# A two-layer relational graph network with two attentions on one core: five places for messages instead of two

## What is computed

```python
def _rgcn_conv(x, src, dst, etype, W, root, b):
    seg = dst * num_rel + etype
    sums = segment_sum(x[src], seg)                      # one sum per node and relation
    cnt = segment_sum(ones, seg)
    mean = sums / maximum(cnt, 1.0)[:, None]
    out = einsum('nri,rio->no', mean, W)                 # 8 relation weights of 768 x 768
    return out + x @ root + b

xn = layernorm(x)
g = _rgcn_conv(relu(_rgcn_conv(xn, ..., W1, root1, b1)), ..., W2, root2, b2)
m = layernorm(xn + performer_attention(xn, 12 heads, 256 features) @ W_proj + b_proj)
x1 = x + g + m
out = x1 + softmax_attention(layernorm(x1))              # 12 heads, qkv with top-2-of-8 low-rank experts
```

## Time and profile before

| | us |
|---|---|
| median of 3 runs | 3865.45 |
| range of the 3 runs | 3851.35 to 3867.41 |
| the profiled execution | 3867.83 |
| its span, first to last instruction | 3865.9 |
| mean granted clock of TensorE in it | 0.946 |
| layer 0, panels (about 52 to 704 from the start of the span) | 650 |
| layer 0, gather (to about 1236) | 530 |
| layer 1, panels (about 1252 to 1853) | 600 |
| layer 1, gather (to about 2396) | 540 |
| both attentions and the join (to the end) | 1470 |

### The profile page before, as it was taken

The page is one execution under the profiler, slowest core; times in us unless marked ns, Lnnn a source line. Parts: engine busy times, 40 slices in busy tenths (PEclk is TensorE's granted clock), DMA queues, the critical chain, the costliest instruction groups (busy, mean ns, idle before and its releaser), DMA issues.

```text
span 3865.9 us, 65243 instructions
## 1 busy us (share of the span) xinstructions
PE 3268.0 (85%) x19556; PEld 2402.3 (62%) x19557; DVE 1775.3 (46%) x2929; ACT 761.7 (20%) x1083; POOL 1258.2 (33%) x1377
## 2 busy tenths in 40 slices
PE   4999999778777998989777777999986887887887
PEld 3877778556555777777555565767654454454454
DVE  5556656444444332322444443343476445355440
ACT  1211211000000221211000001444312442542440
POOL 2740003456564000002456553100140532551451
PEclk9999999999998999999999999999988999999998
DMA  3233333677775223232677775100130000000012
GB/s 123 92 130 111 110 130 101 204 238 241 237 241 166 74 85 102 84 104 72 233 235 242 228 240 184 53 24 12 44 123 27 18 1 17 18 13 6 17 37 72
DMA packets 94889, 434.00 MB, mean 112 GB/s; under 512 B 13615, under 2 KB 13938, under 8 KB 90401
## 3 DMA queue, kind: packets, MB, share of 16 engines
q0 software_dynamic: 55712, 266.87, 21.6%
q1 hardware_dynamic: 36449, 124.02, 9.6%
q10 hardware_dynamic: 2592, 41.29, 2.9%
HBM read 355.21 MB, written 76.88 MB: 112 GB/s over the span
## 4 chain that ended last, share of the span: by engine, by line
PE 46%; DMA 18%; issue 12%; DVE 11%; DVEq 8%; another core or an unknown queue 2%; SPq 2%; ACT 1%; POOL 1%; POOLq 0%; ACTq 0%
DMA msg_table<-MSG 15%; PE PS L1517 10%; PE PS L1406 10%; PE PS L1712 4%; PE PS L1541 3%; PE PS L1646 3%; DVE NM L1329 2%; DVEq L1108 2%; DVE HOT L1108 2%; PE PS L1549 2%; PE PS L1695 2%; DVEq L307 2%; PE PS L1696 1%; PE PS L1586 1%
## 5 line engine op out<-in xcount | busy, mean ns | idle before, releaser
L1517 PE MATMUL PS<-GATA,HOT 128*125 128x384 f16 x2880 | 544.7, 348 | 145.2 <-DVE HOT L1108 74.0
L1406 PE MATMUL PS<-WHL,HT 128*125 (+1 forms) x3240 | 548.9, 332 | 35.2 <-DVE MSG L965 35.0
L1517 PEld LDWEIGHTS PS<-GATA,HOT 128*125 x2880 | 407.8, 145 | 251.5 <-issue 167.8
L1406 PE MATMUL PS<-WHL,XT 128*125 (+1 forms) x3240 | 557.5, 332 | 4.1 <-issue 3.8
L1406 PEld LDWEIGHTS PS<-WHL,HT 128*125 (+1 forms) x3240 | 449.6, 139 | 128.8 <-issue 39.8
L537 POOL DMA_INDIRECT GATA<-msg_table,SKEY x432 | 420.9, 974 | 301.2 <-issue 117.4
L1406 PEld LDWEIGHTS PS<-WHL,XT 128*125 (+1 forms) x3240 | 445.8, 139 | 94.3 <-issue 6.4
L1108 DVE SCALAR_TENSOR_TENSOR HOT<-NODE,DSTF,WHLO x720 | 306.0, 475 | 416.5 <-issue 390.4
L573 POOL TENSOR_TENSOR PL<-PF 125x500 bf16<-125x500 f32 (+1 forms) x360 | 321.0, 926 | 356.7 <-ACT PF L763 353.1
L965 DVE SCALAR_TENSOR_TENSOR MSG<-PS,MSG 125x768 f16<-125x768 f32 x160 | 153.0, 956 | 468.3 <-ACT MSG L606 466.6
L1517 PE MATMUL PS<-GATB,HOT 128*125 128x384 f16 x1440 | 283.0, 357 | 91.1 <-DVE HOT L1108 48.8
(11 more groups left out here) (249 smaller groups left out, 3731.8 us busy)
## 6 DMA issues: line engine op xcount, KB each, us to landing
msg_table<-MSG SPq DMA_DIRECT2D x160, 375.0 KB
WST<-in_wg_dram ACTq DMA_DIRECT2D x17, 2304.0 KB
WST<-in_wf_dram SPq DMA_DIRECT2D x7, 1536.0 KB
KROW<-key_rows POOLq DMA_DIRECT2D x54, 192.0 KB, 3.6
GATA<-msg_table,SKEY POOLq DMA_INDIRECT x432
WST<-in_wm_dram SPq DMA_DIRECT2D x5, 1152.0 KB
ROOT<-in_x_dram SPq DMA_DIRECT2D x10, 375.0 KB
xn_rows<-ROOT SPq DMA_DIRECT2D x10, 375.0 KB
```

Source lines behind the costliest of these rows:

```text
L1406: ins = pe.matmul(PS[0:ROWS, b0 + h, 0:HALF], X[:, xp, k, bass.ts(t, ROWS)], panel_part(slot, wp, k, h), start=k == 0 and xp + wp == 0, st ...
L1517: ins = pe.matmul(PS[0:ROWS, bass.ds(((n + (L + 1)) % 2) * 2 + h, 1), 0:HALF].rearrange("p a c -> p (a c)"), HOT[:, bass.ds((n % 2) * AT + ...
```

## The change

MSG gets five places (`PLACES`), taken by t % 5, and each place has a semaphore of its own for its store. SyncE no longer waits for the landing of a store: it waits for `pair_out`, issues, and goes on. `msg_free` is gone. ScalarE waits itself, for the semaphore of the place that it is to write, to the count that the earlier uses of this place have reached; before the first use of a place in layer 0 it doesn't wait. GpSimd waits for all five semaphores before the gathers. The ten rows of a panel are written out in SyncE's program, where a loop of five turns stood.

```diff
--- before.py
+++ after.py
@@ -29,6 +29,7 @@
 MSG_DOWN = (2.0 ** -16, 2.0 ** -22)
 W_TOP = 2.0 ** 14
 RING = 5
+PLACES = 5
 JSLOT = (0, 1, 2, 3, 4, 5, 0, 3, 4, 5)
 EARLY = 2 * ROWS
 PAIRS = HEADS // 2
@@ -127,7 +128,7 @@
 
         gctx = ExitStack()
         ROOT = sb(gctx, "ROOT", [ROWS, RT, D], f32)
-        MSG = sb(gctx, "MSG", [ROWS, 2, 2 * D], f16)
+        MSG = sb(gctx, "MSG", [ROWS, PLACES, 2 * D], f16)
         cctx = ExitStack()
         KEYHOT = sb(cctx, "KEYHOT", [128, RING, GRP, KHI], bf16)
         LOWHOT = sb(cctx, "LOWHOT", [128, RING, GRP, KLO], bf16)
@@ -205,7 +206,7 @@
         PS = top.enter_context(nc.psum_tensor("PS", [128, 8, 512], f32))
 
         names = """consts_in x_in0 x_in1 stat_done sd_done xn_done xn_stored xt_made t_hi t_free
-            w_in w_max w_row w_top w_all w_scale w_hi w_lo wp_in acc_done pair_out msg_out msg_free bias_in bias_free
+            w_in w_max w_row w_top w_all w_scale w_hi w_lo wp_in acc_done pair_out msg_out0 msg_out1 msg_out2 msg_out3 msg_out4 bias_in bias_free
             edges_in zeros_made bounds_made bounds_t lim_made
             hot1_made hot1_used cnt_done hir_made hir_out key_in0 key_in1 key_in2 key_in3 key_in4 keys_ready low_made relations_made inverse_made rows2_in keys_made counts_found counts_taken
             hot_made gat_in0 gat_in1 gat_in2 gat_in3 gat_in4 gat_in5 gat_in6 gat_in7 gat_in8 gat_in9 gat_in10 gat_in11 pass_done pass_out group_used weights_made msg_hi rows_done
@@ -350,18 +351,13 @@
 
                 def store_messages(p, xn=False):
 
-                    def store(t, j):
+                    for t in range(RT):
                         sp.wait_ge(S["pair_out"], p * RT + t + (ROW_SUMS * L + 3))
-                        sp.dma_start(msg_rows[bass.ts(t, ROWS), bass.ds(p, 1), :].rearrange("n r c -> n (r c)"),
-                                     MSG[:, j, :]).then_inc(S["msg_out"], 16)
+                        sp.sem_inc(S["sp_tick"], 1)
+                        sp.dma_start(msg_rows[t * ROWS:(t + 1) * ROWS, bass.ds(p, 1), :].rearrange("n r c -> n (r c)"),
+                                     MSG[:, t % PLACES, :]).then_inc(S[f"msg_out{t % PLACES}"], 16)
                         if xn:
-                            sp.dma_start(xn_rows[bass.ts(t, ROWS), :], ROOT[:, bass.ds(t, 1), :].rearrange("p a c -> p (a c)")).then_inc(S["xn_stored"], 16)
-                        sp.wait_ge(S["msg_out"], p * (16 * RT) + t * 16 + (L * 16 * REL * RT + 16))
-                        sp.sem_inc(S["msg_free"], 1)
-
-                    with sp.Fori(0, RT // 2) as i:
-                        for j in range(2):
-                            store(i * 2 + j, j)
+                            sp.dma_start(xn_rows[t * ROWS:(t + 1) * ROWS, :], ROOT[:, t, :]).then_inc(S["xn_stored"], 16)
 
                 if L == 0:
                     load_panel(1)
@@ -520,7 +516,8 @@
 
             for L in range(2):
                 edge_weights(L)
-                g.wait_ge(S["msg_out"], 16 * REL * RT * (L + 1))
+                for j in range(PLACES):
+                    g.wait_ge(S[f"msg_out{j}"], 16 * REL * RT // PLACES * (L + 1))
                 g.sem_inc(S["pool_tick"], 1)
                 for t in range(TILES):
                     grp, k = t // AT, t % GSLOTS
@@ -602,8 +599,10 @@
 
             def message_high(L, p, t):
                 act.wait_ge(S["acc_done"], p * RT + t + (ROW_SUMS * L + 2))
-                act.wait_ge(S["msg_free"], p * RT + t + (REL * RT * L + 1))
-                act.activation(halves(MSG[:, t % 2, 0:D]), rowps(2 * (t % 2)), ACT.Copy, scale=MSG_DOWN[L]).then_inc(S["msg_hi"], 1)
+                uses = p * (RT // PLACES) + (t // PLACES + REL * RT // PLACES * L)
+                if L or t >= PLACES or not isinstance(p, int) or p:
+                    act.wait_ge(S[f"msg_out{t % PLACES}"], uses * 16)
+                act.activation(halves(MSG[:, t % PLACES, 0:D]), rowps(2 * (t % 2)), ACT.Copy, scale=MSG_DOWN[L]).then_inc(S["msg_hi"], 1)
 
             def relu(t):
 
@@ -769,7 +768,7 @@
             v.memset(ONEF[:], 1.0)
             v.drain()
             v.sem_inc(S["zeros_made"], 1)
-            for n_, k_ in (("acc_done", 1), ("pair_out", 2), ("msg_free", 2), ("bias_free", 1),
+            for n_, k_ in (("acc_done", 1), ("pair_out", 2), ("bias_free", 1),
                            ("pass_done", 1), ("pass_out", 2), ("counts_taken", 1), ("h_free", 1), ("mix_act", mix.size["act"]), ("mix_dve", mix.size["dve"]), ("mp_free", 2), 
                            ("lg_free", 2), ("ffn_dve", ffn.size["dve"]), ("ffn_act", ffn.size["act"]), ("av_done", PARTED), ("row_in", 16),
                            ("or_free", 2), ("fp_free", 2), ("out_free", 2),  ("xf_free", 2)):
@@ -962,8 +961,8 @@
 
                 def message(p, t):
                     v.wait_ge(S["msg_hi"], p * RT + t + (REL * RT * L + 1))
-                    v.scalar_tensor_tensor(halves(MSG[:, t % 2, D:2 * D]), rowps(2 * (t % 2)), MSG_DOWN[L],
-                                           halves(MSG[:, t % 2, 0:D]), ALU.mult, ALU.subtract).then_inc(S["pair_out"], 1)
+                    v.scalar_tensor_tensor(halves(MSG[:, t % PLACES, D:2 * D]), rowps(2 * (t % 2)), MSG_DOWN[L],
+                                           halves(MSG[:, t % PLACES, 0:D]), ALU.mult, ALU.subtract).then_inc(S["pair_out"], 1)
 
                 def relation_weights():
```

## The result

| | before | after |
|---|---|---|
| median of four runs, us | 3863.61 | 3806.14 (3798.85 to 3811.31) |
| profiled execution, its span, us | 3867.83, 3865.9 | 3807.46, 3805.6 |
| mean granted clock | 0.946 | 0.953 |

The ratio is 0.9855, 95% interval 0.9827 to 0.9883: faster by 1.45%, 57 us. The forecast was 87 us less than before, near 3780. The time measured lies in its outer range (3762 to 3825) and above the forecast's own, 3764 to 3799.

What follows compares the result with a forecast made beforehand. Serial message stores, two places with SyncE waiting for each landing, were taken to bound the panels; 52 + 22 + 6.7 + 6.1 = 87 us off 3867.8, with the median 2.4 lower, gives 3780; range 3762 to 3825.

Steps and rivals of the forecast that it cites:

- Places and the wait; layer 1: Layer 1's panels: with five places ScalarE's wait is over before reached; period becomes 59.0, saving 52 us over seven periods.
- Into panel 2 and panel 3: Layer 0, entries into panels 2 and 3: TensorE's gap and slow work after it go, saving 6.1 and 6.7 us.
- Layer 0, panels 3 to 7: Layer 0: four periods fall from 69.6 to 63.6, with 0.5 us per panel left standing, saving 22 us.
- The load beside more stores: Weight load issued behind row 8's message, with two more stores coming meanwhile: called the unknown, taken as no effect.
- rivals 1 and 4: In 12 panels, load lands 20 us after issue: 3838, chance 0.09; load waits behind all earlier stores: 3985, chance 0.03.
- Rival 2: Panel 1: message and `xn_rows` stores pile up and may overflow five places; 20 us given back, 3800, chance 0.04.
- Rival 3: Nothing moves because something else, VectorE's messages at its panel work, binds just behind the store: 3865, chance 0.02.
- Issues, code, memory; gathers: Same stores in same order, few register instructions on ScalarE, five semaphore waits before gathers, 9 KB more MSG: priced at nothing.

Runs made afterwards that it cites:

- the filled loops of layer 1: Changed kernel with 15, then 28, one-element memsets behind each message in VectorE's loop over layer 1's panels 1 to 7: 3563.43 and 3567.18 us.

## Why the prediction was right and where it was wrong

**Places and the wait; layer 1.** Right, with its size, and the mechanism shown (no store in ScalarE's waits): 52.2 us against 52, by a period of 59.06 against 59.0, and the clock stayed up. What the term did not separate is that two places with waits of their own give this too, and five places with serial stores most of it; 29 us of room were far more than needed. The 2.9 us that the prediction sets against the rows is an estimate by the Trainium skill, DMA: Bandwidth & Descriptors, Anatomy of one DMA, whose formula is for transfers issued by GpSimd. These stores are SyncE's; they took 5.5 us, and the 52 us agree with that.

**Into panel 2 and panel 3.** Right: 6.6 and 6.5 us against 6.1 and 6.7. The gaps and the slow rows behind them went as read from the earlier trace rows.

**Layer 0, panels 3 to 7.** This step failed, with the wrong sign: "69.6 becomes 63.6, the measured period without the gap", 22 us with half a microsecond left standing. It measured +9.5. I took the 63.64 of the earlier trace rows for the period without the stores' gap. It is also the one period in which VectorE's loop makes no turn, and that is what counts: it is 63.66 after, and in the run with five places and serial stores 63.65, and all periods fall to about 63.85 once the turns are gone. The gap of 3.68 us that JUNK released was read as the end of a chain of stores; I looked at the message (436.70) and the counts behind it and not at the row just ahead of them, whose 8.15 us of idle time had no releaser at all. With the turns gone the total comes near the 87 us, 85 on the first chip, but that is not the forecast come true: 14 of the 85 the same edit gave to the kernel before, and the change was worth 71 (3830.23 to 3758.93).

**The total.** That 3806 lies within the range does not bear this term out. The other terms were right and 31.5 us were missing here; of the stages priced at nothing some gave 9 us and some took 4. The range reached to 3825 without a mechanism of its own, and the forecast's own ended at 3799.

**The load beside more stores.** Taken at no effect. TensorE never waited for the load, nor did VectorE in panels 3 to 7, so rivals 1 and 4 did not happen; but the load together with stores that overlap it lengthened the turn from 8.0 to 10.4 us (32.1 and 41.5 us in four turns), which is the 9.5. The load small (7.9), the load a row earlier (8.25) or stores one at a time (8.2): each alone takes most of that away.

**Rival 2**, stores piling up in panel 1, did not happen: panel 1 is 70.51 us after against 77.16. **Rival 3** holds for layer 0, for a cause that it did not name: something stood just behind the store.

**Issues, code, memory; gathers.** Costed at nothing. Small shifts came at places the change does not touch: 1.5 us at the start, 1.7 in panel 0 of layer 1, 7.0 earlier in the second gather. The gathers are what differs most between chips and between runs, so I give these no cause.

**What stays open** is why layer 0's loop is fetched again at every turn and layer 1's is not. Length is not it: the filled loops of layer 1 hold more busy instructions (169 and 299 against 149) and fetch nothing at their turns. No run moved layer 0's loop to another place in VectorE's program, or gave layer 1's the work of layer 0's, so either may decide.

## What to carry to other kernels

Ahead of a row whose releaser is the engine you study, read that engine's own idle time: "issue" with no releaser at the first instruction of a loop's body, once per turn, is a cost of the loop, and writing the loop out removes it; two steps in a turn remove half of the turns. Then look whether packets of an "instruction" queue stand in that idle time. A period "without the gap" may only be used as the goal when it is known which of the gap's causes it lacks. Where two causes meet at one point, remove both: layer 0's period of 69.6 us became 67.7 without the turn, 72.0 without the stores' wait, and 63.9 without either.

## What the runs showed of the hardware

- A turn of an engine's loop cost 7.7 to 10.6 us on VectorE in layer 0, 0.5 us or nothing on VectorE in layer 1 with 20 to 299 busy instructions a turn, some 7 us on TensorE in one attention and none in the other. Where it was dear, packets of instructions moved in the idle time, and it grew by 2.4 us beside a weight load and overlapping stores.
- Stores issued without a wait for the one before kept up with a row of 5.85 us in two places, each 5.5 us alone. Once a panel, beside the weight load, ScalarE waited 5.6 us for one of them, some 10 us after its message, and TensorE did not.
- Between chips the kernel before differs by 6.5% (3863.6 and 3610.9 us), while the changed kernel's panels of layer 1 are 59.06 us on every one. The difference is in the two stages with the gathers. From layer 0's root panel to layer 1's panel 0 the changed kernel took 623.9 us on one chip and 499.7 on another, and from layer 1's root panel to the first attention 576.7 and 460.1: 241 of the 244 us between these two executions.
